# A two-layer gated cross-attention kernel: new order of its first norms and keys, a ternary rounding on VectorE, halves at the end, and attention numerators handled two score groups at a time

## The reference, cut to what matters

```python
x = x + tanh(g_xattn[0]) * xattn_0(layernorm(x), ctx)                 # 16 heads of 16, 77 keys, softmax
x = x + tanh(g_ffn[0])   * bitlinear_ffn(layernorm(x))                # 256 -> 1024 -> 256, ternary weights
x = x + tanh(g_xattn[1]) * xattn_1(layernorm(x), ctx, ctx, distances) # biases; + -log(distances) * |scale|
x = x + tanh(g_ffn[1])   * expert_ffn(layernorm(x))                   # expert 0 only; its own layernorm

def _quant_act(x):      # before both products of bitlinear_ffn, per row
    scale = 127.0 / clip(max(abs(x), axis=-1), EPS)
    return clip(round(x * scale), -128, 127) / scale
```

## Time and profile before

| | |
|---|---|
| median of 3 runs | 415.22 us (414.89 to 416.18) |
| profiled execution | 416.79 us, of which the span of the trace is 415.0 us |
| mean granted TensorE clock | 0.931 of full speed |
| TensorE busy | 328.2 us (79%) in 3254 matmuls |
| VectorE busy | 297.2 us (72%) in 690 |
| ScalarE busy | 283.5 us (68%) in 516 |
| GpSimd busy | 227.9 us (55%) in 408 |
| DMA | 22.02 MB |

### The profile page before, as it was taken

How to read it: one execution, slowest core, us unless ns; L and a number is a source line. 1 busy time by engine, 2 the same in 40 slices (tenths; PEclk the granted TensorE clock), 3 DMA queues, 4 the chain that set the end, 5 groups by cost and what they waited for, 6 DMA issues and landing times.

```text
span 415.0 us, 8997 instructions
## 1 busy us (share of the span) xinstructions
PE 328.2 (79%) x3254; PEld 267.5 (64%) x3254; DVE 297.2 (72%) x690; ACT 283.5 (68%) x516; POOL 227.9 (55%) x408
## 2 busy tenths in 40 slices
PE   3658859787876765877787899898878899999990
PEld 2437648566664443455565788687667799888880
DVE  6685747877886657989986467777856558777775
ACT  4137787899896777988953788866678755555520
POOL 5246555776577411456766655567774155544442
PEclk9695898999899869869998999999999999999997
DMA  8996303111100000310073112211100000000001
GB/s 247 243 165 190 77 26 81 38 40 41 42 3 20 2 0 2 52 23 2 2 227 75 49 51 51 51 37 30 37 2 2 2 2 26 28 28 27 25 27 51
DMA packets 23171, 22.02 MB, mean 53 GB/s; under 512 B 4695, under 2 KB 22488, under 8 KB 23051
## 3 DMA queue, kind: packets, MB, share of 16 engines
q1 hardware_dynamic: 23128, 21.45, 20.9%
HBM read 10.34 MB, written 2.10 MB: 30 GB/s over the span
## 4 chain that ended last, share of the span: by engine, by line
PE 38%; DVE 26%; ACT 16%; issue 9%; POOL 8%; DMA 1%; SPq 0%; ACTq 0%; DVEq 0%; POOLq 0%
PE psA L1681 9%; PE psD L1666 4%; PE psBE L1666 4%; DVE st L865 4%; ACT pp_hi L713 3%; POOL lns L399 3%; DVE ham L1155 3%; PE psD L1370 3%; DVE mx L1109 3%; PE psA L1463 2%; ACT p L704 2%; PE psBE L1396 2%; PE psA L1634 2%; POOL pp_lo L491 1%; DVE o L1094 1%
## 5 line engine op out<-in xcount | busy, mean ns | idle before, releaser
L491 POOL TENSOR_TENSOR pp_lo<-p,pp_hi 124x512 f16<-124x512 f32 x80 | 92.7, 1178 | 45.6 <-ACT pp_hi L713 45.6
L399 POOL TENSOR_TENSOR lns<-lns,mhalf 128x2 f32<-128x2 f32 x40 | 32.2, 805 | 117.0 <-DVE lns L870 116.8
L1109 DVE TENSOR_REDUCE mx<-psBE 128x6 f32<-128x462 f32 (+1 forms) x96 | 54.6, 582 | 31.1 <-PE psBE L1396 30.8
L704 ACT ACTIVATE p<-psD 124x512 f32<-124x512 f32 x80 | 47.6, 597 | 28.7 <-PE psD L1370 26.1
L1370 PE MATMUL psD<-qb,ktb 98*124 98x256 f16 (+1 forms) x256 | 50.1, 293 | 5.7 <-DMA qb<-mT 4.8
L713 ACT ACTIVATE pp_hi<-p 124x512 f16<-124x512 f32 x80 | 50.4, 629 | 0.0
L1370 PEld LDWEIGHTS psD<-qb,ktb 98*124 98x124 f16 (+1 forms) x256 | 33.5, 147 | 10.5 <-DMA qb<-mT 6.8
L1396 PE MATMUL psBE<-kt_hi,q_hi 128*128 128x154 f16 (+2 forms) x160 | 34.2, 283 | 5.0 <-ACT mT L695 3.8
L1681 PE MATMUL psA<-ew_lo,pp_hi 128*128 128x256 f16 x128 | 34.9, 273 | 0.0
L1681 PE MATMUL psA<-ew_hi,pp_lo 128*128 128x256 f16 x128 | 34.9, 273 | 0.0
L1681 PE MATMUL psA<-ew_hi,pp_hi 128*128 128x256 f16 x128 | 34.9, 273 | 0.0
(11 more groups left out here) (201 smaller groups left out, 1013.1 us busy)
## 6 DMA issues: line engine op xcount, KB each, us to landing
qb<-q_hi SPq DMA_DIRECT2D x32, 128.0 KB
xs<-in_x SPq DMA_DIRECT2D x8, 256.0 KB, 4.6
tw_raw<-in_tw SPq DMA_DIRECT2D x2, 1024.0 KB, 11.7
qb<-q_lo SPq DMA_DIRECT2D x16, 128.0 KB
space<-in_ew SPq DMA_DIRECT2D x2, 1024.0 KB, 6.5
out<-space SPq DMA_DIRECT2D x8, 256.0 KB, 2.1
ktb<-km SPq DMA_DIRECT2D x6, 248.0 KB, 9.4
qb<-bT_lo SPq DMA_DIRECT2D x8, 104.0 KB
```

The costliest lines, as they stand in the source:

```text
L399: nc.gpsimd.tensor_tensor(lns[:, n % 4, 1, :], lns[:, n % 4, 0, :], mhalf[:, :], ALU.pow).then_inc(s_rs, 1)
L491: nc.gpsimd.tensor_tensor(pl[:, u % 2, 2 * r:2 * r + 2, :], p32[:, n % 4, :, :], ph[:, u % 2, 2 * r:2 * r + 2, :], ALU.subtract).then_inc( ...
L704: a_(p32[:, n % 4, :, :], psD[n % 2][0:KR, :].rearrange("p (t r) -> p t r", t=2), ACT.Exp, scale=1.0 / SSC).then_inc(a["exp"], 1)
L1109: v.tensor_reduce(pairs[:, MP[k][0]:MP[k][1]:MP[k][2], :], psBE[:, n % 2, 0:hn * KEYS].rearrange("p (q e k) -> p q e k", e=2, k=KEYS), AX. ...
```

## The change

- **Pairs.** `high` (ScalarE) and `plo` (GpSimd) handle two neighbouring groups 2m, 2m+1 at a time (1024 columns, one instruction in place of two); pairs cross the border between units. The exponentials stay single, and exponential n waits for plo of pair n//2 - 2. `high` of a pair follows the exponential of the next even group. On GpSimd the slot's pairs are 2 or 3: in an odd slot the factors stand between the first and the second pair, in an even slot ahead of both. `values` waits for (5u+4)//2 + 1 pairs.
- **Start.** The first queries stand directly behind unit 0's transposes on TensorE, ahead of the transposes of unit 1, which go behind the first queries; ScalarE's copies likewise. VectorE makes statistics and norms of units 0 and 1 ahead of the masks, two of the four key tables there and the other two in attention slots 2 and 3; statistics 2 move from slot 0 to ahead of it. The masking of keys is a function of its own (keys_masked). On SP's queue the key blocks go behind the seven broadcasts.
- **Ternary.** The rounding of tile 1 moves from ScalarE to VectorE (128x1024, with its own semaphore); the value tables' steps move from slots 4 to 7 to slots 7 to 10, with their ones column written for attention 0 only; keys_high tables 2 and 3 of attention 1 move to the first slots of attention 1, table 1 is in slot 4.
- **End.** The last unit's product goes into two PSUM banks, one per tile; sum, statistics, factors, norm and the store are made per half, the first half's sum ahead of the norm of unit 6.

The diff, cut; "..." stands where lines are left out:

```diff
@@ -335,11 @@
...
-    key_blocks(0)
...
+    key_blocks(0)
@@ -371,12 @@
...
-    for u in range(NU):
+    for u in range(NU - 1):
...
-    for i in (0, 1):
-        sp.wait_ge(d_out[i], 16 * NU // 2)
+    u = NU - 1
+    for j in (0, 1):
+        sp.wait_ge(E["out"], u + 1 + j)
+        sp.dma_start(io["out"][u * UR + j * 128:u * UR + (j + 1) * 128, :], y32[:, 1, j, :]).then_inc(d_out[1], 16)
+    sp.wait_ge(d_out[0], 16 * NU // 2)
+    sp.wait_ge(d_out[1], 16 * (NU // 2 + 1))
@@ -424,6 @@
...
+    def factors_half(j):
+        n = 5 * NU - 1
+        g = lns[:, n % 4, :, j:j + 1]
+        pool.wait_ge(s_var, n + 1 + j)
+        nc.gpsimd.tensor_tensor(g[:, 1, :], g[:, 0, :], mhalf[:, 0:1], ALU.pow).then_inc(s_rs, 1)
+        pool.wait_ge(s_rs, n + 1 + j)
+        link(nc.gpsimd.tensor_tensor(g[:, 2, :], g[:, 1, :], g[:, 1, :], ALU.mult))
+        link(nc.gpsimd.tensor_tensor(g[:, 3, :], g[:, 0, :], g[:, 2, :], ALU.mult))
+        link(nc.gpsimd.tensor_scalar(g[:, 4, :], g[:, 3, :], -0.5, 1.5, ALU.mult, ALU.add))
+        nc.gpsimd.tensor_tensor(g[:, 5, :], g[:, 4, :], g[:, 1, :], ALU.mult).then_inc(E["fac"], 1)
@@ -480,24 @@
...
-    def plo(l, u, r):
-        a = A[l]
-        if not 0 <= u < NU:
-            return
-        n = 5 * u + r
-        pool.wait_ge(a["phi"], n + 1)
+    def plo(l, m):
+        a, u = A[l], (2 * m + 1) // 5
+        pool.wait_ge(a["phi"], m + 1)
...
-        nc.gpsimd.tensor_tensor(pl[:, u % 2, 2 * r:2 * r + 2, :], p32[:, n % 4, :, :],
-                                ph[:, u % 2, 2 * r:2 * r + 2, :], ALU.subtract).then_inc(a["plo"], 1)
+        nc.gpsimd.tensor_tensor(pair(plf, m), p32[:, 2 * m % 4:2 * m % 4 + 2, :, :].rearrange("p n t r -> p (n t r)"),
+                                pair(phf, m), ALU.subtract).then_inc(a["plo"], 1)
...
-        plo(l, s - 2, 2)
-        if 0 <= s - 4 < NU:
-            factors_act((1 + 2 * l) * NU + s - 4, (1.0, SX)[l], A[l]["fac"])
-        for u, r in ((s - 2, 3), (s - 2, 4), (s - 1, 0), (s - 1, 1)):
-            plo(l, u, r)
+        for n in range(5 * s - 8, 5 * s - 3):
+            if n % 2 == 1 and 0 <= n < 5 * NU:
+                plo(l, n // 2)
+            if n == 5 * s - 8 and 0 <= s - 4 < NU:
+                factors_act((1 + 2 * l) * NU + s - 4, (1.0, SX)[l], A[l]["fac"])
@@ -592,11 @@
...
-    tables_k(0)
...
+    tables_k(0)
...
-    ln0_transposed(1)
@@ -700,17 @@
...
-            ge(act, a["plo"], n - 3)
+            ge(act, a["plo"], n // 2 - 1)
...
-    def high(l, u, r):
-        a, n = A[l], 5 * u + r
-        if 0 <= u < NU:
-            act.wait_ge(a["exp"], n + 1)
+    def high(l, m):
+        a, u = A[l], (2 * m + 1) // 5
+        if 0 <= m < 5 * NU // 2:
+            act.wait_ge(a["exp"], 2 * m + 2)
...
-            a_(ph[:, u % 2, 2 * r:2 * r + 2, :], p32[:, n % 4, :, :], ACT.Copy).then_inc(a["phi"], 1)
+            a_(pair(phf, m), p32[:, 2 * m % 4:2 * m % 4 + 2, :, :].rearrange("p n t r -> p (n t r)"),
+               ACT.Copy).then_inc(a["phi"], 1)
@@ -723,7 @@
...
-                high(l, *((u, k - 1) if k > 0 else (u - 1, 4)))
+                if (5 * u + k) % 2 == 0:
+                    high(l, (5 * u + k) // 2 - 1)
@@ -765,7 @@
...
-                    act.wait_ge(f["q1"], 2 * u)
+                    act.wait_ge(f["q1"], u)
+                    act.wait_ge(f["q1b"], u)
@@ -784,12 @@
...
-            for j in (0, 1):
-                n = 2 * u + j
-                act.wait_ge(f["amax"], u + 1)
-                ge(act, f["phT"], n - 3)
-                a_(hq[u % 2][:, j, :], h32[:, j, :], ACT.Identity, scale=ham[:, 2, j:j + 1],
-                   bias=epsc[:, 4:5]).then_inc(f["q1"], 1)
+            act.wait_ge(f["amax"], u + 1)
+            ge(act, f["phT"], 2 * u - 3)
+            a_(hq[u % 2][:, 0, :], h32[:, 0, :], ACT.Identity, scale=ham[:, 2, 0:1],
+               bias=epsc[:, 4:5]).then_inc(f["q1"], 1)
@@ -817,6 @@
...
+    ln0_transposed(1)
@@ -895,6 @@
...
+    def keys_masked(l):
@@ -927,8 @@
...
-        i.then_inc(s_vo, 1)
-        v.tensor_scalar(vo[:, b, hf, :, :, HD], vm[:, :, :], SM * SONE, None, ALU.mult).then_inc(s_vo, 1)
+        i.then_inc(s_vo, 1 + l)
+        if l == 0:
+            v.tensor_scalar(vo[:, b, hf, :, :, HD], vm[:, :, :], SM * SONE, None, ALU.mult).then_inc(s_vo, 1)
@@ -951,17 @@
...
-    ln0_stats(0)
-    ln0_stats(1)
-    ln0_apply(0, refine(0, SX))
...
+    ln0_stats(0)
+    ln0_stats(1)
+    ln0_apply(0, refine(0, SX))
+    ln0_apply(1, refine(1, SX))
...
-    ln0_apply(1, refine(1, SX))
-    for i in range(4):
+    for i in range(2):
...
+    keys_masked(0)
+    ln0_stats(2)
@@ -970,10 @@
...
-        if (s, r) in ((0, 2), (0, 3), (0, 5), (1, 1), (1, 5), (2, 1)):
-            ln0_stats({(0, 2): 2, (0, 3): 3, (0, 5): 4, (1, 1): 5, (1, 5): 6, (2, 1): 7}[s, r])
-        if (s, r) == (0, 1):
-            queries_lo(0, 0)
+        if (s, r) in ((0, 2), (0, 5), (1, 1), (1, 5), (2, 1)):
+            ln0_stats({(0, 2): 3, (0, 5): 4, (1, 1): 5, (1, 5): 6, (2, 1): 7}[s, r])
+        if (s, r) in ((2, 3), (3, 4)):
+            keys_high(0, s)
@@ -1157,15 @@
...
-            ge(dve, f["q1"], 2 * u)
+            ge(dve, f["q1"], u)
...
+            dve.wait_ge(f["amax"], u + 1)
+            ge(dve, f["phT"], 2 * u - 2)
+            v.tensor_scalar(hq[u % 2][:, 1, :], h32[:, 1, :], g[:, 2, 1:2], MAGICQ, ALU.mult, ALU.add).then_inc(f["q1b"], 1)
...
-        if 4 <= s < 8:
-            if s == 4:
+        if 7 <= s < 11:
+            if s == 7:
...
-            tables_v(1, s - 3)
+            tables_v(1, s - 6)
@@ -1209,6 @@
...
+    def expert_sum_half(j):
+        e, u = E, NU - 1
+        n = 4 * NU + u
+        y = y32[:, u % 2, j, :]
+        if j == 0:
+            dve.wait_ge(e["half"], 1)
+            dve.wait_ge(e["xb"], u + 1)
+            dve.wait_ge(d_out[u % 2], 16 * (u // 2))
+        else:
+            dve.wait_ge(e["pm2"], u + 1)
+        acc = acc_(u)[:, 0:D] if j == 0 else psX[:, D:2 * D]
+        link(v.scalar_tensor_tensor(y, xnk[:, 2 * u + j, :], SY / SX, acc, ALU.mult, ALU.add))
+        link(v.bn_stats(st[:, n % 4, j, :], y))
+        link(v.bn_aggr(mv[:, n % 4, j, :], st[:, n % 4, j, :]))
+        v.tensor_scalar(lns[:, n % 4, 0, j:j + 1], mv[:, n % 4, j, 1:2], EPS * SY * SY, None,
+                        ALU.add).then_inc(s_var, 1)
+    def expert_norm_half(j):
+        e, u = E, NU - 1
+        n = 4 * NU + u
+        y = y32[:, u % 2, j, :]
+        dve.wait_ge(e["fac"], u + 1 + j)
+        link(v.scalar_tensor_tensor(y, y, mv[:, n % 4, j, 0:1], gg[:, :], ALU.subtract, ALU.mult))
+        dve.wait_ge(e["xgb"], u + 1)
+        v.scalar_tensor_tensor(y, y, lns[:, n % 4, 5, j:j + 1], xgb[:, u % 2, j, :],
+                               ALU.mult, ALU.add).then_inc(e["out"], 1)
@@ -1223,6 @@
...
+    queries_lo(0, 0)
@@ -1232,18 @@
...
+            keys_masked(1)
...
-        if s < 7:
-            keys_high(1, s - 3)
+        if s == 4:
+            keys_high(1, 1)
...
+    keys_high(1, 2)
...
+    keys_high(1, 3)
@@ -1264,9 @@
...
-    for u in (NU - 2, NU - 1):
-        expert_sum(u)
-        expert_norm(u)
+    expert_sum(NU - 2)
+    expert_sum_half(0)
+    expert_norm(NU - 2)
+    expert_sum_half(1)
+    for j in (0, 1):
+        expert_norm_half(j)
@@ -1322,7 @@
...
-            ge(pe, F["xTl"], k)
+            ge(pe, F["xTl"], k + 3)
@@ -1341,7 @@
...
-    ln0_transposes(1)
@@ -1406,8 @@
...
-            pe.wait_ge(a["phi"], 5 * u + 5)
-            pe.wait_ge(a["plo"], 5 * u + 5)
+            pe.wait_ge(a["phi"], (5 * u + 4) // 2 + 1)
+            pe.wait_ge(a["plo"], (5 * u + 4) // 2 + 1)
@@ -1609,7 @@
...
-                pe.wait_ge(f["q1"], n + 1)
+                pe.wait_ge((f["q1"], f["q1b"])[j], u + 1)
@@ -1617,8 @@
...
-        if 4 <= s < 8:
-            tables_vo(1, s - 4)
+        if 7 <= s < 11:
+            tables_vo(1, s - 7)
@@ -1637,8 @@
...
-            if u < 4:
-                pe.wait_ge(s_vo, 8 + 2 * u + 1)
+            if 3 <= u < 7:
+                pe.wait_ge(s_vo, 8 + 2 * (u - 3) + 1)
@@ -1674,17 @@
...
+        last = u == NU - 1
...
-            o = acc_(u)[:, j * D:(j + 1) * D]
+            o = (psX if last and j == 1 else acc_(u))[:, j * D:(j + 1) * D]
...
-                           start=(j == 0 and c == 0 and x_ == 0 and w_ == 0),
-                           stop=(j == 1 and c == FK - 1 and x_ == 1))
+                           start=((last or j == 0) and c == 0 and x_ == 0 and w_ == 0),
+                           stop=((last or j == 1) and c == FK - 1 and x_ == 1))
+            if last and j == 0:
+                i.then_inc(e["half"], 1)
...
+    ln0_transposes(1)
```

## The result

The changed kernel takes **460.15 us** (median of 4 runs, 458.78 to 467.9) against 415.06 for the kernel before in the same runs: ratio 1.107, 95% interval 1.102 to 1.113. The forecast was 433.6 us with a range of 420 to 441. The sign was right, and the loss is 45.1 us where 18.4 were forecast.

A forecast was written before the change was run, and what follows sets the result against it. In the second attention no engine was taken as full; a chain of waits through four engines set the time. Pairs +25.1, start -4.5, ternary -2.5 and end +0.3 gave +18.4 on 415.2, so 433.6 us, range 420 to 441.

The forecast's parts named there:

- +2.9: Even attention slots with queries (4 and 6): factors' end to q_hi grows from 2.37 to 5.25 us; four slots, +11.6.
- +0.3: End of the kernel: halves wait for GpSimd's addition, norm 6 stands behind it; +0.3 us, bounds -1.5 and +1.5.
- the ternary terms: Ternary stretch: tables and keys_high leave VectorE's slots, one rounding comes in; sum -2.5 us, bounds -6 and +1.5.
- +25.1 forecast: Both attentions: sum of the pairs' costs over even, odd, last and early slots, in us.
- the turn: Slots 2 and 3: ring of exponent, copy and subtraction, 4.1 us for two groups; +2.5 taken of at most 4.5.
- The pair ahead of the factors can start 1.6 us into the slot (exponent, pair copy) and ends by 3.9: Odd slot 5: this pair hardly pushes the factors, which began 4.0 us behind the residual.
- The two added steps and two keys_high in the first slots of attention 1 lie in VectorE's gaps: First slots of attention 1: the moved work fits VectorE's gaps of 1 to 2 us, so no cost was added.
- -4.5: Start: head start of the first queries, in us; bounds -8.8 and 0 (the DMAs decide).
- Rival 5: Start: DMAs, with the broadcasts ahead, hold the first scores and nothing is won; 438.1 us, chance 0.06.
- (2): Attention slots: same mechanism at half its price, through statistics ready sooner or slack in TensorE's order; 421.1 us, chance 0.18.
- (3): Attention slots: pairs cost nothing, since factors run before the pair's copy is done; faster, 408.5 us, chance 0.10.
- (4): Four slots with ew_lo: VectorE stands behind GpSimd's longer subtractions, 1.1 us more each; 438.1 us, chance 0.08.

The follow-up runs named there:

- pairs_only: The kernel before with the paired copies and subtractions alone; 454.4 us, ratio 1.094.
- pairs_early_copy: pairs_only with each pair's copy directly behind its second exponential, ahead of the next one; 438.3 us, ratio 1.055.
- tables_only: The kernel before with the value tables' steps moved to slots 7 to 10 and keys_high of attention 1 moved as in the change; 421.4 us, ratio 1.014.
- tables_behind: tables_only with TensorE's table step behind the ternary transposes of its slot, no longer ahead of them; 418.1 us, ratio 1.0034.
- all_but_pairs: The changed kernel with single copies and subtractions and the factors' place as before; 422.8 us, ratio 1.017.
- round_only: The kernel before with the rounding of tile 1 on VectorE alone; 421.6 us, ratio 1.014.
- experiment 6: pairs_only with early copy, factors behind the first pair in even slots, and each pair's subtraction in two instructions; 426.4 us, ratio 1.024.

## Why the prediction was right and wrong

**What held.** The change is slower, and the mechanism that the forecast named is there: the factors ahead of a pair that ScalarE's exponential waits for. It is one of two causes, and the smaller. A pair's subtraction takes 2.18 us (2.25 forecast), its copy 1.05, the pairs save nothing, and ScalarE idles 3.76 us ahead of the fourth exponential of slot 4. In pairs_only, even slots with queries are 2.8 and 2.4 us longer in attention 1 and 2.2 and 1.9 in attention 0, against +2.9; with the factors behind the first pair, 1.5 and 2.9 of it come back in attention 1. The stretch of the expert FFN kept its length. The last rows of the end:

```profile
446.36 1.26 POOL L552 TENSOR_TENSOR tw_raw<-tw_raw,orow 128x512 f32<-128x512 f32 x1
```

```profile
447.72 0.42 DVE L1257 SCALAR_TENSOR_TENSOR space<-tw_raw,psA 128x256 f32<-128x256 f32 x1 [4.38 <-POOL tw_raw L552]
...
448.93 0.87 DVE L1279 SCALAR_TENSOR_TENSOR space<-space,mv,bc 128x256 f32<-128x256 f32 x2
...
450.63 0.41 DVE L1257 SCALAR_TENSOR_TENSOR space<-tw_raw,psA 128x256 f32<-128x256 f32 x1
...
454.36 0.48 DVE L1270 SCALAR_TENSOR_TENSOR space<-space,lns 128x256 f32<-128x256 f32 x1
```

The first half's sum starts when GpSimd's addition is done, its sum and statistics take 1.28 us (1.25 forecast), norm 6 stands behind it, and the rest of the kernel is 0.2 to 0.3 us longer: +0.3 was right, with some luck, as the forecast's own terms (413.2 - 412.4 - 0.3) give +0.5. The other slips are as small: slot 8's terms give +3.7 and not +3.6, and the ternary terms are not added up to the -2.5 that they are given.

**The step that failed in the pairs** (+25.1 forecast, 37.3 of span measured). The forecast had the turn in its hands ("the ring of exponent 0.5, copy 1.0 and subtraction 2.25 plus waits comes to 4.1 us for two groups"; measured 3.84), but used it for slots 2 and 3 alone, and there took +2.5 of at most 4.5. The two stretches that hold those slots lost 4.4 and 5.6, together 10.0: that term was mis-sized by 7.5. The bound of 4.5 was wrong too. It compared the turns' throughput with the slot's length and left out that the values, the next maxima and with them the next slot come later as well. The rest, 4.0, is attention 1 (+15.3, where the terms give +11.3). For the odd slot the way from the factors to q_hi was priced rightly (+1.4; the chain shows +1.3), but the step "The pair ahead of the factors can start 1.6 us into the slot (exponent, pair copy) and ends by 3.9" failed: it started at 3.2, since the slot before hands on late `values` and so late scores, run at a lower clock. Slot 5 got +3.3 and slot 7 +2.5 instead of +0.5. In attention 0 the sum came out right (11.7 against 11.3), but by luck: slots 5 and 7 got +3.9 instead of +1.9, slots 4 and 6 +4.1 instead of +5.8. The forecast also had no term for TensorE's clock, which in pairs_only is 0.93 in attention 1 where it was 1.00, with 4.0 us more of TensorE's busy time. pairs_early_copy shows the turn to be the larger cause: without it, the early slots and slot 5 of attention 1 are at their old length.

**The step that failed in the tables** ("The two added steps and two keys_high in the first slots of attention 1 lie in VectorE's gaps": 0 forecast, +8.6 measured). VectorE had gaps (in tables_only it idles 4.40 us ahead of 213.67). But a table step is also an instruction of TensorE, with a wait for VectorE's last work of the slot before, and it was moved ahead of the transposes on which the end of the ternary chain hangs. The forecast counted the moved step on one of its two engines. tables_behind shows the order on TensorE to be 3.7 of the 8.6 us, the lower clock behind its waits included; the remaining 4.9 were read from the trace (product behind the table, transposes behind the last table) but not taken apart further.

**The rounding.** Its duration was right in the mean (1.0 taken, 1.07 measured in all_but_pairs, from 0.75 to 1.67), and the periods of the later ternary slots in all_but_pairs (7.4, 6.7 and 7.2 us, against 8.7, 7.7 and 7.7) are near the forecast 6.7. But these gains are the tables' going: in round_only the stretch grew by 4.0. From first to last row maxima, all_but_pairs is 1.3 us shorter where 2.5 were forecast; the 2.3 us behind it had no term at all.

**The start** was over-forecast: 2.3 to 2.4 us in the trace and none that the medians show, against -4.5. Rival 5 had the reason: the first scores wait for a DMA, which takes 4 us longer than before. Not the seven broadcasts alone are in question there, but all that the DMA engines carry at the time (share 1.11).

**The rivals.** (2) and (3) fell: no wait overlapped in the kernel's favour. (4) fell where it was placed: ew_lo takes 1.22, 1.73, 1.22 and 1.21 us in its four slots, less in all than before (1.22, 1.67, 1.67 and 1.35). The stall that it names is there, on additions of VectorE (up to 2.08 us instead of 0.17) and on its rounding, but shortening it gave nothing back (experiment 6). The range missed because its upper end was made of small terms of the same mechanism (+27, the ports) and held no case in which turns govern every slot. Of the 23.7 us between forecast and measured span change, 12.2 are the pairs, 12.4 the rest of the change (5.7 instead of -6.7), and -0.9 their overlap.

## What to carry to other kernels

- When single steps become pairs over the same buffers, count the distance between a step's wait and the step it waits for, in instructions of that engine's order. Here it went from three groups to one pair; copy and subtraction then took turns, and the sum of their times, 3.84 us a pair, governed the slots.
- A copy that stands behind the next producer step inherits that step's wait. Put it ahead, and the wait is off its path: here that gave 16 us back.
- Of a step that is moved, list the instruction on each engine with its wait, and what is queued behind each. A gap on one engine says nothing of the other.

## What was not expected of the hardware

The clock went down with the waits. The mean granted clock of the profiled execution fell from 0.931 to 0.900 of full speed. In tables_only TensorE idled 3.52 us ahead of 199.34 and 2.49 us ahead of 207.28; behind these waits the same 16 matmuls took 3.27 and 3.62 us and not 1.91, so that waits cost it more than their length.

VectorE stood still until a GpSimd instruction ended, and GpSimd the other way round. Its addition of 128x2 numbers took 1.44 us beside a long subtraction, 0.17 without. Its rounding of 128x1024 took 0.75 us alone, and 0.93, 1.41 or 1.67 where the GpSimd instruction that ran at its start ended 0.38, 0.85 or 1.12 us into it; GpSimd's 128x512 addition (L533 of all_but_pairs), begun while a rounding waited or ran, took 1.71 us instead of 1.27.
